# Expert layers of a graph network: routing that also finds the node of each slot, gathers inside the experts' stage, and fetching merged with what follows it

## The reference, cut to what matters

```python
scores = rows @ gate_w + gate_b          # third: a small network in place of one matrix
pick 2 of 16 (first), 1 of 8 (second, at most ceil(1.25*3125/8) = 489 nodes an expert), 2 of 6 (third)
y = func(rows @ w1[e] + b1[e]) @ w2[e] + b2[e]     # third: one more 256x256 layer between
first:  x = x + layernorm(rows + sum(weight * y)) * gamma + beta
second: x = x + clean(weight * y)        # NaN -> 0, +inf -> 1e4, -inf -> -1e4
third:  x = x + sum(weight * y)          # and x is the output
```

## Time and profile before

| | us |
|---|---|
| median of 3 runs | 7942.77 (7941.25 to 7955.9) |
| the profiled execution | 7951.78 |
| its span | 7950.2 |
| PE busy in it | 4464.4 (56%) |
| DVE busy | 3856.6 (49%) |
| POOL busy | 3287.4 (41%) |
| mean granted TensorE clock | 0.733 of full speed |

### The profile page before, as it was taken

The page is one execution under the profiler, slowest core; times in us unless marked ns, Lnnn a source line. Parts: engine busy times, 40 slices in busy tenths (PEclk is TensorE's granted clock), DMA queues, the critical chain, the costliest instruction groups (busy, mean ns, idle before and its releaser), DMA issues. The chain is left out here.

```text
span 7950.2 us, 67396 instructions
## 1 busy us (share of the span) xinstructions
PE 4464.4 (56%) x16661; PEld 3136.4 (39%) x16661; DVE 3856.6 (49%) x7877; ACT 2058.4 (26%) x4299; POOL 3287.4 (41%) x2886
## 2 busy tenths in 40 slices
PE   6699655438347750411117476985774864555263
PEld 3466433337235530200016343764553753333152
DVE  3244466411356556399953687226664025443212
ACT  4577200002123220321212111222331214444110
POOL 0666677331327740035530264005773024773313
PEclk8799777679767665655558698996675986666586
DMA  5233433446335541100030121004553534653254
GB/s 152 87 104 103 91 91 91 101 120 185 104 94 139 136 106 33 29 0 0 0 67 10 27 46 39 12 18 111 139 140 82 181 116 133 183 180 76 73 153 115
DMA packets 566098, 729.01 MB, mean 92 GB/s; under 512 B 197250, under 2 KB 424673, under 8 KB 562600
## 3 DMA queue, kind: packets, MB, share of 16 engines
q1 hardware_dynamic: 397770, 382.70, 17.2%
q0 software_dynamic: 168080, 343.54, 15.9%
HBM read 554.94 MB, written 174.38 MB: 92 GB/s over the span
## 5 line engine op out<-in xcount | busy, mean ns | idle before, releaser
L601 PE MATMUL ps<-msg,same 128*125 128x256 f32 (+2 forms) x3328 | 1354.2, 554 | 865.3 <-issue 325.4
L601 PEld LDWEIGHTS ps<-msg,same 128*125 128x125 f32 x3328 | 775.4, 261 | 1292.7 <-issue 697.5
L577 POOL DMA_INDIRECT msg<-d_gat,src_i x832 | 888.2, 1068 | 349.2 <-issue 232.8
L577 POOL DMA_INDIRECT msg<-d_lin,src_i x416 | 441.4, 1061 | 269.4 <-issue 120.8
L577 POOL DMA_INDIRECT msg<-rel_rows,src_rel x416 | 426.7, 1026 | 189.3 <-issue 116.1
L491 POOL DMA_INDIRECT rec<-rec,slot_i x391 | 412.8, 1056 | 193.0 <-issue 109.7
L1166 POOL DMA_DIRECT2D answered<-y x90 | 102.9, 1143 | 874.4 <-DVE y L1153 831.0
L1831 POOL TENSOR_TENSOR xc<-xc,dA 128x1250 f32<-128x1250 f32 x80 | 307.9, 3849 | 346.6 <-DVE dA L1899 346.6
L1844 PE MATMUL ps<-parts,sel 96*128 96x512 bf16 x320 | 97.9, 461 | 610.8 <-DVE dA L1899 489.1
L427 PE MATMUL ps_f<-w,hs 128*128 128x256 f32 x1568 | 393.1, 407 | 74.5 <-DVE hs L466 65.1
L1128 ACT ACTIVATE hid<-ps_h,b 128x250 f32<-128x250 f32 x380 | 178.2, 469 | 973.2 <-PE ps_h L1093 973.2
(11 more groups left out here) (551 smaller groups left out, 9096.6 us busy)
## 6 DMA issues: line engine op xcount, KB each, us to landing
lo_rows<-lo_r SPq DMA_DIRECT2D x208, 256.0 KB
fil<-rec SPq DMA_DIRECT2D x104, 512.0 KB
w<-in_L_ffn_w SPq DMA_DIRECT2D x80, 512.0 KB
w<-in_L_ffn_w SPq DMA_DIRECT2D x40, 1024.0 KB
rows<-sent SPq DMA_DIRECT2D x93, 250.0 KB
answered<-y POOLq DMA_DIRECT2D x90, 250.0 KB
rel_rows<-row SPq DMA_DIRECT2D x25, 896.0 KB
lo_rows<-ffn_lo_r SPq DMA_DIRECT2D x64, 250.0 KB
```

Of the source, the lines that this page charges most:

```text
L577: nc.gpsimd.indirect_dma_start(msg[:, g % R, j, :], None, table, bass.IndirectOffsetOnAxis(idx[:, n:n + 1], 0)).then_inc(msg_in[g % R], 16)
L601: nc.tensor.matmul(ps[:, j, 0:width], same[:, g % 2, j, :], msg[:, g % R, j, 0:width], start=True, stop=True).then_inc(mm, 1)
```

## The change

`normalise_all` has no clearing any more. `gates` stores the normalised rows as they are into a table `tokens` (3125 rows), by SP, and waits for it. `most_blocks` takes the capacity into account. `route` also inverts the slots: for each choice DVE makes one-hot tiles of the slot within its half block (125 wide) and of the half block (HB = 2 x blocks wide), once multiplied by the tile number and once by the partition number plus one, in bf16; 25 matmuls per choice sum them to the node of every slot, and four closing operations write `token_i`. `send_rows` is gone. In `block_experts` POOL gathers the rows of block n+2 from `tokens`, one indirect DMA for each 125 slots, ahead of the store of block n; the store is split at partition 112. SP only loads weights. POOL's loop is written out. `fetch_rows` goes by groups of 5 tiles with a ring of 10, and does the norm, the clean-up or the store of the output for each group as it comes.

```diff
-def most_blocks(chosen, n_exp, rows=N):
-    return (chosen * rows + n_exp * (BR - 1)) // BR
+def most_blocks(chosen, n_exp, capacity=None):
+    blocks = (chosen * N + n_exp * (BR - 1)) // BR
+    if capacity:
+        blocks = min(blocks, n_exp * ((capacity + BR - 1) // BR))
+    return blocks + blocks % 2
```

In `gates`, on SP behind the loads:

```diff
+                for to, of in also:
+                    for lo, hi in SPLIT:
+                        sp.dma_start(to[lo:hi], of[lo:hi]).then_inc(moved, 16)
+                if also:
+                    sp.wait_ge(moved, 32 * len(also))
```

In `route`, on PE, and on DVE for each choice and at the end:

```diff
+                for q in range(chosen):
+                    pe.wait_ge(marked, q + 1)
+                    for t in range(NT):
+                        ins = nc.tensor.matmul(ps_who[:, 0:2 * HB], at_row[:, q, t, :], who[:, q, t, :, :].rearrange("p v h -> p (v h)"),
+                                               start=q == 0 and t == 0, stop=q == chosen - 1 and t == NT - 1)
+                ins.then_inc(found, 1)
...
+                    split_index(nc, c, slot[:], half[:], low[:], whole_i[:])
+                    c.link(nc.vector.tensor_scalar(low[:], low[:], 1.0, None, ALU.add))
+                    c.step(nc.vector.tensor_tensor(at_row[:, q, :, :], low[:].unsqueeze(2).to_broadcast([P, NT, P]), k.ramp_r1[0:P, :].unsqueeze(1).to_broadcast([P, NT, P]), ALU.is_equal))
+                    c.link(nc.vector.tensor_tensor(at_half[:], half[:].unsqueeze(2).to_broadcast([P, NT, HB]), ramp_h[:].unsqueeze(1).to_broadcast([P, NT, HB]), ALU.is_equal))
+                    c.step(nc.vector.tensor_tensor(who[:, q, :, 0, :], at_half[:], k.ramp_t[0:P, :].unsqueeze(2).to_broadcast([P, NT, HB]), ALU.mult))
+                    c.link(nc.vector.tensor_scalar(who[:, q, :, 1, :], at_half[:], k.ramp_p1[0:P, :], None, ALU.mult))
+                    dve.sem_inc(marked, 1)
...
+                dve.wait_ge(found, 1)
+                c.link(nc.vector.tensor_scalar(token[:], ps_who[:, 0:HB], float(P), None, ALU.mult))
+                c.link(nc.vector.tensor_tensor(token[:], token[:], ps_who[:, HB:2 * HB], ALU.add))
+                c.link(nc.vector.tensor_scalar(token_i[:, 0:HB], token[:], -1.0, 0.0, ALU.add, ALU.max))
```

In `block_experts`, SP loses its first and its per-block row load, and POOL becomes:

```diff
-                        load_rows(1 - b, n + 1)
...
+                def gather(n):
+                    pool.wait_ge(t_mm, n + 1)
+                    for t in range(TB):
+                        nc.gpsimd.indirect_dma_start(rows[:, n % 2, t, :], None, table, bass.IndirectOffsetOnAxis(token_i[:, TB * n + t:TB * n + t + 1], 0)).then_inc(rows_in[n % 2], 16)
+
+                gather(0)
+                gather(1)
                 pool.wait_ge(made, 1)
+                for lo, hi in SPLIT:
+                    for b in range(2):
+                        pool.dma_start(result[blocks * BR + b * P + lo:blocks * BR + b * P + hi, :], zero[lo:hi, :]).then_inc(stored[b], 16)
+                for n in range(blocks):
+                    if n + 2 <= blocks:
+                        gather(n + 2)
+                    pool.wait_ge(o_done, 2 * n + 6)
+                    to = result[n * BR:(n + 1) * BR, :].rearrange("(t p) f -> p t f", p=P)
+                    for lo, hi in SPLIT:
+                        pool.dma_start(to[lo:hi], y[lo:hi, n % 2, :, :]).then_inc(stored[n % 2], 16)
```

`fetch_rows` weighs a group (both choices of 5 tiles), then measures it (norm) or cleans it; the shift of group g-1 and the scaling and adding of group g-2 follow in the same round, and ACT applies the norm between them. The beta pass over x stands at the stage's start. For the third layer SP stores each group's five tiles of x, split at 112, when its last weighing is done:

```diff
+                for g in range(GROUPS + 2):
+                    if g < GROUPS:
+                        weigh(g)
+                        if norm:
+                            measure(g)
+                        if clean:
+                            cleaned(g)
+                    if norm and 1 <= g <= GROUPS:
+                        shifts(g - 1)
+                    if norm and g >= 2:
+                        add(g - 2)
```

More of the change, by code:

```diff
@@ L760, in first_of_max, with gates @@
     c.link(nc.vector.tensor_tensor(onehot, ramp, wide(pick), ALU.is_equal))
-def gates(k, cols, gate, n_exp, w, bias, mode, router=None, scores=None, choice=None):
+def gates(k, cols, gate, n_exp, w, bias, mode, router=None, scores=None, choice=None, also=()):
     nc = k.nc
@@ new lines, in _ @@
+            @block.scalar
+            def _(act):
+                if norm:
+                    for g in range(GROUPS):
+                        act.wait_ge(var, g + 1)
+                        nc.scalar.activation(veps[:, span(g)], veps[:, span(g)], ACT.Sqrt).then_inc(sd, 1)
+                        act.wait_ge(shifted, g + 1)
+                        for t in range(g * STEP, (g + 1) * STEP):
+                            nc.scalar.activation(rows[:, t, :], rows[:, t, :], ACT.Identity, bias=shift[:, t:t + 1], scale=rstd[:, t:t + 1]).then_inc(normed, 1)
@@ new lines, in measure @@
+                def measure(g):
+                    for t in range(g * STEP, (g + 1) * STEP):
+                        c.step(nc.vector.bn_stats(stats[:, t, :], rows[:, t, :]))
+                    c.wait()
+                    for t in range(g * STEP, (g + 1) * STEP):
+                        c.step(nc.vector.bn_aggr(mv[:, t, :], stats[:, t, :]))
+                    c.wait()
+                    nc.vector.tensor_scalar(veps[:, span(g)], mv[:, span(g), 1], EPS, None, ALU.add).then_inc(var, 1)
@@ L1032, in block_experts @@
+def block_experts(k, table, token_i, result, block_i, x, blocks):
     nc = k.nc
@@ L2280, in _, with routed @@
                 k.nc.vector.memset(gate[:], 1.0).then_inc(done, 1)
[L2283 removed]
+def routed(k, rows, n_exp, chosen, x, gate_w, gate_b, mode, capacity=None, norm=None, clean=None, out=None, **more):
     nc = k.nc
[L2286 to L2307 removed]
@@ new lines, in routed @@
+    answered = k.answered[0:(blocks + 1) * BR, :]
+    tensor = lambda n, shape, dt=F32: nc.sbuf_tensor(f"{n}_{x.f}_{n_exp}", shape, dt)
+    with tensor("wt", [P, chosen, NT]) as wt, tensor("slot_i", [P, chosen, NT], I32) as slot_i, \
+            tensor("token_i", [P, 2 * blocks + 2], I32) as token_i, tensor("block_i", [1, blocks], I32) as block_i:
+        with tensor("oh", [P, chosen, NT, n_exp]) as oh:
+            with nc.sbuf_tensor(f"cols_{x.f}_{n_exp}", [128, 2, N], F32) as cols:
+                normalise_all(k, rows, cols)
+                gates(k, cols, None, n_exp, gate_w, gate_b, mode, choice=(oh, wt), also=[(k.tokens.rearrange("(t p) f -> p t f", p=P), rows[:])], **more)
+            route(k, (oh, wt), slot_i, block_i, token_i, n_exp, chosen, blocks, capacity)
+        block_experts(k, k.tokens, token_i, answered, block_i, x, blocks)
+        fetch_rows(k, answered, slot_i, wt, chosen, rows, norm, clean, out)
```

216 lines of the change are left out of this document (95 added, 121 removed).

## The result

The changed kernel takes 7576.4 us (median of 4 runs, 7560.6 to 7576.7), the kernel before 7942.0 (median of 4, 7935.4 to 7955.9): ratio 0.953, 95% interval 0.9515 to 0.955. The forecast was 7538, with 7493 to 7632 around it. The profiled execution took 7576.5 us, its span is 7574.8; the span of before was 7950.2.

The account below looks back on a forecast made before the run. Bound by barrier-separated stage lengths, many nearly idle, then by five engines serving 125-partition transfers in layer 1. Terms sum to -404.5: 7951.8 profiled becomes 7547.3, less 9.0 gives 7538 us, eight in ten 7493 to 7632.

Parts of the forecast that it names:

- the 0.38: Experts' stage: DMA engine share for 5 us after a weight burst, at 120 GB/s, read as 125-partition transfers having five engines.
- Clearing, sending, blocks, start: Gains of 40.8 us (clearing), 207.3 (sending), 58.4 (layer 2's four fewer blocks) and 6 (start of the experts' stage).
- Routing: Inverting the slots on DVE and TensorE after the gates adds 60 us over three layers, bounds 50 and 75.
- The forecast's form: Experts' stage, layer 1: two blocks need 8.5 us to the weights' issue plus 7.5 landing, 16 together, 8.0 a block.
- the last weight tile lands some 6.5 to 7.5 us after its issue: Experts' stage: with the worst engine loaded 5.0 of 7.9 us the backlog goes; gains 47 us (layer 1), 45 (layer 3).
- beside the first gathers: Fetch of layer 1: norm's beta pass moves there, leaving 13 of 41 us behind the last gather, gain 28 us.
- The estimate of 12 us that stood with the rule: Fetch: if DVE shuts GpSimd out, 0.1 us more on 125 gathers takes 12 us off; left out of the sum.
- A: Whole kernel: the forecast itself, 7538 us, inner bounds 7500 to 7590; chance 0.65.
- B: Experts' stage: weights land as late as now, so 47 + 45 + 6 us are not gained, 7636; chance 0.22.
- The rule that the forecast cited against splitting: Experts' stage: transfers to disjoint partitions serialise, so the split store gains nothing; cited under B.
- D: Experts' stage: gathers become the pace and the kernel is slower than before, 7943 us and more; chance 0.02.
- C: All better: landing under 6.9 us, TensorE at 7.7 and 7.0 a block, routing +50: 7489 us; chance 0.10.

Follow-up runs that it names:

- run 2: Changed kernel with a block's answer stored whole by one 125-partition transfer instead of two split at partition 112: 7680.7 us.
- run 6: Kernel before with only the row load and the answer split at partition 112, b2 whole: 7692.9 us, for 7771.7 unchanged on that chip.
- run 1: Changed kernel with only the broadcast load of bias b2 split at partition 112: 7561.9 us.
- run 3: Changed kernel with a block's two gathers replaced by one plain read of 250 consecutive rows, split at partition 112: 7602.6 us.
- run 12: Changed kernel with POOL's gathers issued in mid-block, before its wait for the running block's answer: 7359.7 us, ratio 0.950 to the kernel before.
- run 10: Changed kernel with both repairs, two semaphores for a block's weights and layer 1's beta pass in the gates' stage: 7491.8 us, ratio 0.945 to the kernel before.
- run 4: Changed kernel with norm's beta pass of layer 1 moved from the fetch to the gates' stage: 7566.5 us.
- run 5: Kernel before with only layer 2's blocks capped by the capacity, 16 in place of 20: 7701.8 us, for 7771.7 unchanged on that chip.

## Why the prediction was right, and where it was not

**What bounds it.** Right in the main. Stages that the change leaves alone kept their length to 5.5 us, so stage lengths could be added. That 125-partition transfers have few engines is shown from both sides (runs 2 and 6), and the splits are worth all that the change gained in the blocks of layers 1 and 3. But the forecast read more into the 0.38: that b2, rows and answer share the same five engines, 189 KB on each, 7.9 us. They do not. The queues of the kernel before in layer 3, from 7641.25 to 7643.25 us, while SP's queue q1 moves the last weights, b2 and rows and POOL's q0 the answer:

```profile
q1 hardware_dynamic: 260, 0.21, 30.7%
q0 software_dynamic: 54, 0.17, 29.7%
```

Each keeps about five engines busy, and together they keep 9.7, not 5; over all blocks of that stage the packets give 4.9 and 5.0 engines, 4.5 to 6 us after the first weights' issue. So a transfer of 125 partitions is slow because it has five engines, and the sum of such transfers on one set of five is a step that the trace does not bear out; that it came to 7.9 of the block's 9.13 us was no proof.

**Clearing, sending, blocks, start.** Right to 1 us each: 40.7, 207.3, 59.0 and 6.3. `tokens` goes out under the gates' matmuls, as the forecast named its cover: the gates' stage and routing together grew by 24.0, 10.5 and 19.3 us, less than what routing was given alone.

**Routing.** 53.8 for 60, within 50 to 75. The two wide operations per choice took what was put in (2.24 and 1.25 us in layer 1 for 2.2 and 1.2), the 25 matmuls of a choice 3.6 and 3.3 us for the bound of 5.3. Layer 3 gave most of the difference: 19.3 for 23.

**Experts' stage.** This is the step that was mis-sized. The forecast's form holds: two blocks need 8.5 us and the landing, and with the measured 8.4 that is (8.5 + 8.4)/2 = 8.45 us a block; measured are 339.0/40 = 8.47. With the landings of runs 1, 3, 6 and 12 it is 4 to 7 us short of layer 1's length, and 12 and 15 short where TensorE waits longest (the kernel before and run 2). (Of its own two bounds, 8.0 and 7.94 us a block, the forecast took the smaller, 318 us; the larger gives 320.) The term that failed is "the last weight tile lands some 6.5 to 7.5 us after its issue". It came from dividing the worst engine's bytes by the length of a block: 5.0 us of 7.9, so no backlog. But TensorE does not wait for a mean load, it waits for the last packet of one burst, and the change put more into that burst. The timeline of one block of the changed kernel:

```profile
1660.88 0.39 SPq L1152 DMA_DIRECT2D w<-in_L_ffn_w  x1
1661.01 1.35 POOL L1260 DMA_DIRECT2D answered<-y  x2 [3.49 <-DVE y L1238]
...
1662.48 0.42 SPq L1158 DMA_DIRECT2D b<-in_L_ffn_b  x1
1662.65 1.26 POOL L1246 DMA_INDIRECT rows<-tokens,token_i  x1 [0.30 <-issue]
...
1664.22 1.22 POOL L1246 DMA_INDIRECT rows<-tokens,token_i  x1 [0.30 <-issue]
...
1669.39 3.64 PE L1178 MATMUL ps_h<-xT,w 128*128 128x250 f32 x16 [1.20 <-DMA b<-in_L_ffn_b]
```

and the windows of the same block:

```profile
1661.00:1662.00 1.00, 1.00 (x7) 0.89 (x6) 0.00 (x0) 0.47 (x1) 0.99 (x2) 1.00 0.13 14
1662.00:1666.00 4.00, 3.79 (x20) 3.18 (x19) 0.68 (x1) 1.41 (x3) 2.83 (x3) 1.00 1.01 294
1666.00:1669.00 3.00, 2.19 (x11) 1.56 (x9) 0.85 (x2) 0.00 (x0) 0.05 (x1) 1.00 0.55 167
```

Weights, answer and rows, 1.65 MB, are all issued within 5 us; 1.1 us pass before the engines are busy, 4 us run at the full share of all engines, then 3 us at 0.55, and the layer starts 8.5 us after the first issue. In the kernel before, the rows were loaded in mid-block. Runs 1, 6 and 12 each take one thing out of that tail (b2's few engines, the rows' place) and land after 7.5, 7.8 and 7.4 us in layer 1: 324.3, 330.3 and 324.3 us, nearer to the forecast's 318. That the tail holds both is shown for layer 1 by runs 1 and 12, the second with the reserve for its chip. In layer 3 neither moved the landing (8.0 and 8.2 us); there only the second semaphore took the wait away, and which transfer makes it stays open. The sign that the forecast named, waits for the last weight tile under 10 us, did not come: they were 20.8 and 23.5 us. The forecast noted where the gathers go in POOL's order, and used it only for when the rows are ready, not for what they ride with.

In layer 3 the same formula with the measured 7.9 gives (7.7 + 7.9)/2 = 7.8 us, 234 in all, and 244.4 were measured. Part of the rest is seen in three block starts of the changed kernel:

```profile
7305.38 2.73 PE L1178 MATMUL ps_h<-xT,w 128*128 128x250 f32 x8 [2.43 <-DMA b<-in_L_ffn_expert_b]
...
7313.67 1.85 PE L1178 MATMUL ps_h<-xT,w 128*128 128x250 f32 x8
7314.48 0.39 SPq L1152 DMA_DIRECT2D w<-in_L_ffn_expert_w  x1
...
7323.20 3.45 PE L1178 MATMUL ps_h<-xT,w 128*128 128x250 f32 x8 [2.47 <-DMA b<-in_L_ffn_expert_b]
```

and the windows of these three groups of matmuls, with the granted clock:

```profile
7305.38:7308.11 2.73, 2.73 (x10) 2.22 (x11) 0.00 (x0) 0.47 (x1) 2.42 (x2) 0.69 0.96 276
7313.67:7315.52 1.85, 1.85 (x11) 1.63 (x10) 0.42 (x1) 0.47 (x1) 0.92 (x2) 1.00 0.01 3
7323.20:7326.65 3.45, 3.45 (x9) 2.73 (x10) 0.00 (x0) 0.47 (x1) 2.43 (x2) 0.54 0.96 307
```

After a wait of 2.4 us the same 8 matmuls take 2.73 or 3.45 us in place of 1.85, at a granted 0.69 and 0.54 in place of 1.00. The block that starts at 7305.38 takes 8.3 us where the forecast had 7.0, and the next weights are issued 9.1 us after its start, not 7.7. The stage's granted clock is 0.97 (0.99 in run 10), its PE busy time 195.9 us (184.9 in run 10). The forecast priced the wait and left out what a wait does to the work behind it.

**Fetching.** Layer 1: the tail is as worked out (13.2 us from the last weighing at 2059.7 to the next stage, forecast 13), but 6.3 us were lost where DVE's beta pass held up a gather (run 4). The forecast put the pass "beside the first gathers", and from 1.26 us for a gather beside short DVE work read that overlap is free. What it weighed against this came in another form: the Trainium skill, "SBUF — State Buffer", section "Who interferes with whom", describes an exclusive lock between DVE and GpSimd for a whole instruction; the trace agrees, with 7.64 us for one gather beside a pass of 6.83. The forecast took from it DVE's two-port modes only, and the pass is a tensor_tensor. The same section expects a tensor_tensor with both inputs in SBUF to hold up only GpSimd work that reads SBUF; whether a gather's reading of its indices is that was not tried. The estimate of 12 us that stood with the rule was for 0.1 us on every gather; what came was one long stall. Layer 2 gave 27.7 for 24 (bounds 18 to 30), with DVE busy 54.1 of 65.0 us as foreseen, and layer 3 12.6 for 8: 5.3 us pass from the start of the last weighing to the end, in place of 15.9.

**Rivals.** The result lies between the numbers of A and B, inside A's inner bounds (7500 to 7590): in layer 1 the landing fell from 9.2 to 8.4 us, by half of what A needs. That it lies so near is in part luck, since 44 us too few in some parts met 15 too many in others. B's reason for doubt, that issue, transfer and completion set the time and not the few engines, was half right for the changed kernel, since its full-share phase alone is 4 us. The rule that the forecast cited against splitting does not carry over: in the Trainium skill, "DMA: Bandwidth & Descriptors", section "Rules for kernel authors", it is about disjoint partition halves that both spray across all 16 engines. A whole store of 125 partitions kept 5.1 engines busy, and run 2 is 104 us slower without the split. D did not come: TensorE never waited for rows in the blocks of layers 1 and 3, apart from the first. The stage lengths of C (7.7 and 7.0 us a block) were nearly reached in the repaired kernel (7.8 and 7.1), by waiting for less and not by its landing under 6.9 us.

**The numbers.** In spans the gain is 29 us short of the forecast: 33 from the blocks of layers 1 and 3, 5.5 each from the fetch of layer 1 and from stages left alone, less some 15 that routing, the other fetches and the small terms gave back. The other 9 of the 38 us between 7538 and 7576 are the step from profile to median: the profiled run of before stood 9.0 us above its median, the one of after at it. Subtracting one execution's excess from another's forecast was no better than leaving it.

## What to carry to other kernels

A consumer that waits for one counter of several transfers waits for the last packet of the whole burst, so what matters is not the mean load of the engines but what else is issued in those microseconds and how far the last transfer spreads; give the parts that are needed first a semaphore of their own, which here took 27.7 and 28.9 us off the changed kernel's two stages, where its two rearrangements of the transfers (runs 1 and 12) took off 14.7 and 14.7 in layer 1 and 3 to 4 in layer 3. When a transfer is moved, ask what it now travels with, and not only when it must be there. Before two engines are overlapped, look for a long single instruction on one of them: a median of short overlaps says nothing about it.

## What the runs showed of the hardware that was not expected

- Chips differ more than the runs of one: the same kernel took 7944.1, 7926.8, 7771.7 and 7745.6 us on four. In the profile of before layer 1's blocks start at 1703.1 us, in run 5, on the third chip, at 1593.5: 110 us lie ahead of them.
- A transfer of 125 partitions kept about five engines busy, on either queue (4.8 and 4.9 at the same time, in the kernel before); two such transfers from different queues did not share one set of five.
- A gather on POOL took 7.64 us beside a DVE addition of 6.83 us with both inputs in SBUF, and 1.20 us alone; beside DVE additions of 1.48 us up to 2.37.
- A store of 250 KB from 125 partitions, whole in place of 112 and 13, lengthened 40 blocks by 43.6 us and 30 blocks by 45.3, although the same bytes moved.
- TensorE's 1440 matmuls of layer 1 took 303.8 us in the stage without waits and 326.0 in the one with most, at granted clocks of 0.99 and 0.95.
